# Turning the experts' gated rows through a DRAM scratch and VectorE's 32x32 transposes, with down products two blocks behind

## Chip, cores and metric

One core of one Trainium2 chip runs the kernel, which is written directly for the engines, each with its own instruction list and semaphores. The metric is the device time of one execution in microseconds (us). TensorE (PE) multiplies, VectorE (DVE) and ScalarE (ACT) work element by element, GpSimd (POOL) does small work and software-made transfers, and SyncE (SP) issues transfers.

## Reference, cut to what matters

Two layers follow each other on x (64 batches of 64 tokens, 512 features). The first picks a 64x64 matrix per batch and applies a gated feed-forward net whose weights come from splines. The second adds adapters and a mixture of 8 experts, of which each of the 4096 tokens uses 2:

```python
router_logits = x_flat @ gate_w.T
top_w, sel = jax.lax.top_k(router_logits, TOPK)          # TOPK = 2
top_w = jax.nn.softmax(top_w, axis=-1)
tw = jnp.zeros((n, E)).at[tok_ids, sel].add(top_w)
g = jnp.einsum('nd,efd->enf', x_flat, gate_proj)         # E = 8, F_DIM = 352, D = 512
u = jnp.einsum('nd,efd->enf', x_flat, up_proj)
h = jax.nn.silu(g) * u
eo = jnp.einsum('enf,edf->end', h, down_proj)
out = jnp.einsum('end,ne->nd', eo, tw)
...
x = x + ffn_2(adapters(x))
```

Only the experts' part is touched by the change.

## The kernel before, in words

The first stages (up to about 680 us) compute the first layer, the adapters and the router, and write each token's row, its token number and its two shares to `rows_dram`, sorted by expert. The last stage, `experts`, goes over 71 blocks (`BLOCKS`) of 128 rows. A block has one expert. Its weights sit in one of three `slots`; SP loads the next expert into a slot that is done with.

For block j the work is:

- ACT issues four transfers of the block's rows, `fetch_z(j)` (L1823), four blocks ahead. The rows arrive so that DVE's transpose of 32x32 squares, `turn(j)` (L1881), writes the turned block to a bank.
- The turned block is split into a rounded high part (`high_z`, L1844, ACT) and a low rest (`low_z`, L1885, DVE).
- PE does `gate_up(j)` (L1760): 24 products of 352 columns, in three passes (high by high, high by low, low by high), into the banks GATE and UP.
- ACT takes the silu of GATE (`gate`, L1838), and DVE multiplies it with UP into `hid` (`multiply`, L1894).
- PE turns `hid` by three products with the identity (`transpose_h`, L1773) into the bank HT; ACT and DVE split HT (`high_h` L1834, `low_h` L1889).
- PE does `down(j)` (L1781): 9 products of 512 columns. It comes after `gate_up(j+1)`, so it lags by one block.
- DVE reads the small tile `meta` (L1828 fetches it), computes the block's share (`set_share`, L1900, three tiny operations) and weighs the result (`weigh`, L1911). POOL adds it to `out` by an indirect transfer (`scatter`, L1732), one at a time.

Each engine works in the order of its own `body`. For ACT (L1848) this is `high_h(j-1)`, `high_z(j+1)`, `gate(j)`, `fetch_z(j+4)`, `fetch_meta(j)`. For DVE (L1920) it is `low_h(j-1)`, `turn(j+1)`, `low_z(j+1)`, `multiply(j)`, `set_share(j-1)`, `weigh(j-1)`. For PE (L1802) it is `transpose_h(j-1)`, `gate_up(j)`, `down(j-1)`. A wait in such a list holds back all that stands behind it on that engine; on ACT this covers its transfers too, since the same queue issues them.

Of the kernel before, what the change touches and what calls it, by code (L numbers as in the profile page):

```python
# [16 lines left out]
P = 128  # L17
# [42 lines left out]
FC = 3  # L60
# [182 lines left out]
def build(nc, io):  # L243
    kc = {k: v for k, v in io.items() if k.startswith("c_")}
    dram = lambda n, s, d=F32: nc.dram_tensor(n, s, d, kind="Internal").ap()
    late_dram = [dram(f"late_dram{l}", [P, NT, TILE_W]) for l in range(2)]
    rows_dram = dram("rows_dram", [NE * REGION * P, WIDE])
# [6 lines left out]
    with top:  # L254
# [132 lines left out]
        experts(nc, alloc, sem, psum, ident, small, idle, slots, weights_loaded, load_expert, rows_dram, out,  # L387
# [1270 lines left out]
def experts(nc, alloc, sem, psum, ident, small, idle, slots, weights_loaded, load_expert, rows_dram, out,  # L1658
# [3 lines left out]
    with ExitStack() as scope:  # L1662
        sb = alloc(scope)
        z_quads = [sb(f"z_quads{r}", [P, QUADS, P]) for r in range(AHEAD)]
        meta = [sb(f"meta{b}", [P, META]) for b in range(2)]
# [4 lines left out]
        silu_g, hid = sb("silu_g", [P, FD]), sb("hid", [P, FP])  # L1670
        ht_hi, ht_lo = sb("ht_hi", [P, FC, P], F32R), sb("ht_lo", [P, FC, P], F32R)
# [5 lines left out]
        z_loaded, meta_loaded = [sem(f"ex_z_loaded{r}") for r in range(AHEAD)], [sem(f"ex_meta_loaded{b}") for b in range(2)]  # L1677
        z_turned, zt_high, zt_low, ht_high, hid_set = (sem(n) for n in ("z_turned", "zt_high", "zt_low", "ht_high", "hid_set"))
        part_set, share_set, scatter_set, added = (sem(n) for n in ("part_set", "share_set", "scatter_set", "added"))
# [4 lines left out]
        def quads(zt):  # L1684
            return zt[:, :, :].rearrange("p k (a n) -> p k a n", a=QUADS)
# [8 lines left out]
        with nc.Block() as block:  # L1694
            @block.sync
            def _(sp):
# [8 lines left out]
                for e in range(SLOTS, NE):  # L1705

                    blocks = sp.value_load(ctl[0:1, END_AT + e - SLOTS:END_AT + e - SLOTS + 1], min_val=1, max_val=BLOCKS)
                    sp.wait_ge(filled[HT], blocks + 1)
# [3 lines left out]
                for b in range(2):  # L1712
                    sp.wait_ge(meta_loaded[b], 16 * ((BLOCKS - b + 1) // 2))
# [3 lines left out]
            def _(pool):  # L1717
                nc.gpsimd.memset(hid[:, :], 0.0).then_inc(hid_set, 1)
# [8 lines left out]
                def set_scatter(j, n, b):  # L1727
                    pool.wait_ge(meta_loaded[b], 16 * (n + 1))
                    alone()
                    nc.gpsimd.tensor_copy(scatter_at[b][:, :], meta[b][:, 0:1]).then_inc(scatter_set, 1)  # L1730

                def scatter(j, n, b, first):  # L1732

                    if not first:
                        pool.wait_ge(added, 16 * j)
                        alone()
# [3 lines left out]
                    alone()  # L1740
# [14 lines left out]

            @block.tensor
            def _(pe):
                pe.wait_ge(hid_set, 1)

                def gate_up(j, b, slot):  # L1760

# [226 lines left out]
```

## Time and profile before

| | |
|---|---|
| median of 3 runs | 1149.09 us (1147.99 to 1153.04) |
| the profiled execution, its own time | 1151.42 us |
| its span, first to last instruction | 1149.7 us |
| PE, DVE, ACT, POOL busy | 92%, 60%, 41%, 57% of the span |
| `experts`, first to last `transpose_h` | 691.0 to 1134.5 us |

The page gives busy times for the whole span, a mean over stages with different limits. The change touches the last stage alone, so this stage's own rows are the ones to read: its period for each block, what each engine does in a period, and where it waits. In the rows a `q` behind an engine's name (ACTq) marks instructions that its queue issues; for a transfer the duration is that of the issue, not of the data's way.

### The profile page before, as it was taken

To read this page: it belongs to the slowest core of one execution; us is meant where nothing else is said; L and a number is where in the kernel's file an instruction comes from. 1 tells how busy PE (TensorE), PEld (TensorE's weight loads), DVE (VectorE), ACT (ScalarE), POOL (GpSimd) and SP (SyncE) were. 2 spreads that over 40 slices of the span, in tenths; PEclk is the share of its full clock that TensorE was granted. 3 is DMA by queue.
4 is the path that set the end of the run, shared out by engine and by line. 5 is a ranking of instruction groups with operands and counts; after the bars stand their busy time and mean duration, and the time that the engine had idled before them with its cause. 6 is when DMAs were issued, how large, how long until landed. Compare 5 with 4: busy or idle time off the path is not lost. (4 is left out here: it accounts for less than half of the span.)

```text
span 1149.7 us, 35580 instructions
## 1 busy us (share of the span) xinstructions
PE 1056.2 (92%) x12060; PEld 977.3 (85%) x12061; DVE 692.7 (60%) x1478; ACT 474.0 (41%) x964; POOL 653.4 (57%) x889
## 2 busy tenths in 40 slices
PE   2679999999999999779999929999999999999995
PEld 1679999999999999669999928998999999999994
DVE  8946666677766666447566715555555555555553
ACT  3246767777766776433334212222222222222221
POOL 6568999999999999403646322333333333333333
PEclk9758999999999999869999959999999999999998
DMA  6053554555555455346878567586767676754454
GB/s 260 1 163 123 187 180 163 199 201 176 186 194 180 164 184 167 126 145 196 278 244 266 163 212 190 82 238 122 198 124 196 130 190 136 185 91 78 87 82 65
DMA packets 126611, 188.31 MB, mean 164 GB/s; under 512 B 26040, under 2 KB 89656, under 8 KB 123104
## 3 DMA queue, kind: packets, MB, share of 16 engines
q1 hardware_dynamic: 57408, 130.43, 33.9%
q0 software_dynamic: 16432, 36.78, 16.4%
q10 hardware_dynamic: 52736, 20.64, 7.4%
q8 instruction: 21, 0.34, 0.1%
q14 instruction: 14, 0.11, 0.0%
HBM read 108.37 MB, written 81.83 MB: 165 GB/s over the span
## 5 line engine op out<-in xcount | busy, mean ns | idle before, releaser
L1725 POOL TENSOR_TENSOR idle<-small 128x1 f32<-128x1 f32 x212 | 70.8, 337 | 275.9 <-DMA out<-result,scatter_at 191.5
L1768 PE MATMUL banks<-slots,zt_hi 128*128 x568 | 189.6, 334 | 22.2 <-DVE zt_lo L1887 22.2
L1770 PE MATMUL banks<-slots,zt_lo 128*128 x568 | 184.3, 325 | 0.0
L1769 PE MATMUL banks<-slots,zt_hi 128*128 x568 | 184.3, 325 | 0.0
L962 POOL TENSOR_TENSOR in_lo<-inner,in_hi 128x512 fp32r<-128x512 f32 x128 | 164.5, 1292 | 29.9 <-ACT in_hi L1110 29.6
L1199 DVE TENSOR_TENSOR inner<-silu,banks 128x512 f32<-128x512 f32 x128 | 87.9, 687 | 112.9 <-ACT silu L1105 109.9
L1836 ACT ACTIVATE ht_hi<-banks 128x384 fp32r<-128x384 f32 x71 | 35.0, 493 | 254.9 <-PE banks L1778 247.6
L1741 POOL DMA_INDIRECT out<-result,scatter_at x71 | 111.7, 1573 | 28.1 <-issue 26.4
L1768 PEld LDWEIGHTS banks<-slots,zt_hi 128*128 128x128 f32 x568 | 107.8, 190 | 22.4 <-issue 22.4
L956 POOL TENSOR_TENSOR f_lo<-f_sum,f_hi 128x256 fp32r<-128x256 f32 x128 | 110.9, 887 | 3.8 <-ACT f_hi L1101 3.8
L1105 ACT ACTIVATE silu<-banks 128x512 f32<-128x512 f32 x128 | 76.3, 596 | 76.9 <-PE banks L1031 75.7
L1769 PEld LDWEIGHTS banks<-slots,zt_hi 128*128 128x128 f32 x568 | 107.9, 190 | 0.0
L1770 PEld LDWEIGHTS banks<-slots,zt_lo 128*128 128x128 f32 x568 | 107.8, 190 | 0.0
L1110 ACT ACTIVATE in_hi<-inner 128x512 fp32r<-128x512 f32 x128 | 80.5, 629 | 40.9 <-DVE inner L1199 36.3
L1917 DVE TENSOR_TENSOR result<-banks,share 128x512 f32<-128x512 f32 x71 | 49.1, 691 | 75.9 <-DMA out<-result,scatter_at 51.4
L1031 PE MATMUL banks<-f_hi,gu_hi 64*128 64x256 f32 x512 | 87.4, 336 | 5.9 <-DVE inner L1199 3.0
L1788 PE MATMUL banks<-slots,ht_hi 128*128 x213 | 84.2, 395 | 1.3 <-DVE ht_lo L1891 1.3
L1189 DVE TENSOR_REDUCE f_sum<-banks 128x256 f32<-128x512 f32 x128 | 82.1, 682 | 5.3 <-PE banks L1017 4.9
L1790 PE MATMUL banks<-slots,ht_lo 128*128 x213 | 84.4, 396 | 0.0
L1047 PE MATMUL banks<-in_hi,down_hi 32*128 32x256 f32 x1024 | 83.7, 316 | 0.6 <-POOL in_lo L962 0.6
L1789 PE MATMUL banks<-slots,ht_hi 128*128 x213 | 84.0, 394 | 0.0
L1846 ACT ACTIVATE zt_hi<-banks 128x512 fp32r<-128x512 f32 x72 | 43.1, 599 | 92.2 <-DVE banks L1883 92.1
(255 smaller groups left out, 3148.7 us busy)
## 6 DMA issues: line engine op xcount, KB each, us to landing
late_dram<-split_part SPq DMA_DIRECT2D x32, 816.0 KB, 5.1
slots<-late_dram SPq DMA_DIRECT2D x24, 1088.0 KB, 5.9
z_quads<-rows_dram ACTq DMA_DIRECT2D x286, 64.0 KB, 3.3
raw_part<-in_late_w SPq DMA_DIRECT2D x16, 816.0 KB
x_t<-in_x_t SPq DMA_DIRECT2D x16, 512.0 KB, 3.6
x_both<-in_x_tok SPq DMA_DIRECT2D x16, 512.0 KB, 5.8
x_both<-in_x_res SPq DMA_DIRECT2D x16, 512.0 KB, 3.3
x1t_dram<-x_both SPq DMA_DIRECT2D x16, 512.0 KB, 6.0
```

Of the source, the lines that this page charges most:

```text
L956: nc.gpsimd.tensor_tensor(f_lo[:, g, :], f_sum[g % F_SUMS][:, :], f_hi[:, g, :].bitcast(F32), ALU.subtract).then_inc(f_done, 1)
L962: nc.gpsimd.tensor_tensor(in_lo[:, cs, :], inner[u % 2][:, :, :], in_hi[:, cs, :].bitcast(F32), ALU.subtract).then_inc(in_done, 1)
L1031: ins = nc.tensor.matmul(gu_bank[:, h, m * TILE:(m + 1) * TILE], w[rows, m, cols], f[rows, u, :], start=(i == 0), stop=(i == 2))
L1047: ins = nc.tensor.matmul(out_bank[r][:, cols], w[rows, c, :], x[rows, c, :], start=(c == 0 and i == 0), stop=(c == IC - 1 and i in (2, 4)) ...
L1199: nc.vector.tensor_tensor(inner[u % 2][:, :, :], silu[u % 2][:, :, :], gu_bank[:, :, TILE:2 * TILE], ALU.mult).then_inc(gu_drained, 1)
L1741: nc.gpsimd.indirect_dma_start(out, bass.IndirectOffsetOnAxis(ap=scatter_at[b][:, 0:1], axis=0), result[b][:, :], None, compute_op=ALU.add ...
L1768: nc.tensor.matmul(psum[bank][:, 0:FD], zt_hi[b][:, k, :], w_high, start=(k == 0), stop=False)
L1769: nc.tensor.matmul(psum[bank][:, 0:FD], zt_hi[b][:, k, :], w_low, start=False, stop=False)
L1770: ins = nc.tensor.matmul(psum[bank][:, 0:FD], zt_lo[b][:, k, :], w_high, start=False, stop=(k == DK - 1))
L1788: nc.tensor.matmul(psum[OUT[b]][:, :], ht_hi[:, f, :], w_high, start=(f == 0), stop=False)
L1789: nc.tensor.matmul(psum[OUT[b]][:, :], ht_hi[:, f, :], w_low, start=False, stop=False)
L1790: ins = nc.tensor.matmul(psum[OUT[b]][:, :], ht_lo[:, f, :], w_high, start=False, stop=(f == FC - 1))
```

## The change

`hid` no longer goes through PE. ACT stores it to a scratch in DRAM (`store_h`, 128 x 4 pieces of 96 numbers, 384 bytes each), POOL reads it back in another order (`read_h`, 128 pieces of 1536 bytes), and DVE turns it in 32x32 squares into the bank HT (`turn_h`). Then `high_h` and `low_h` split it as before. The scratch, `hid`, `hid_quads`, `ht_hi` and `ht_lo` have two buffers each, `meta` four. `down` lags `gate_up` by two blocks, `weigh` by three. For the rows to come in the order that this needs, `quads` now writes `zt_hi` and `zt_lo` with "(n a)" where "(a n)" stood: neighbours in a write lie four numbers, 16 bytes, apart. The same holds for `ht_hi` and `ht_lo` (`h_quads`). The down weights' rows are reordered on the host to fit.

```diff
+    hid_dram = dram("hid_dram", [2, QUADS, P, FC * QUAD])
...
         def quads(zt):
-            return zt[:, :, :].rearrange("p k (a n) -> p k a n", a=QUADS)
+            return zt[:, :, :].rearrange("p k (n a) -> p k a n", a=QUADS)
+        def turned_h():
+            return psum[HT][:, 0:FP].rearrange("p (a f n) -> p a f n", a=QUADS, f=FC)
+        def h_quads(ht):
+            return ht[:, :, :].rearrange("p f (n a) -> p a f n", a=QUADS)
...
# GpSimd
+                def read_h(j, n, b, first):
+                    if not first:
+                        pool.wait_ge(h_turned, j - 1)
+                    pool.wait_ge(hid_stored[b], 16 * (n + 1))
                     alone()
+                    nc.gpsimd.dma_start(hid_quads[b][:, :], hid_dram[b].rearrange("q (n a) w -> (q n) (a w)", a=QUADS)).then_inc(hid_loaded[b], 16)
...
# TensorE
-                def transpose_h(j):
-                    pe.wait_ge(drained[UP], j + 2)
-                    pe.wait_ge(drained[HT], j + 1)
-                    for f in range(FC):
-                        ins = nc.tensor.transpose(psum[HT][:, f * P:(f + 1) * P], hid[:, f * P:(f + 1) * P], ident[:, :])
-                    ins.then_inc(filled[HT], 1)
...
                 def body(j, n, b):
-                    last, now = slot_of(j - 1), slot_of(j)
+                    last, now = slot_of(j - 2), slot_of(j)
                     wait_weights(j)
-                    transpose_h(j - 1)
                     gate_up(j, b, now)
-                    down(j - 1, n - 1 + b, 1 - b, last)
+                    down(j - 2, n - 1, b, last)
...
# ScalarE
+                def store_h(j, n, b, first):
+                    act.wait_ge(drained[UP], j + 2)
+                    if not first:
+                        act.wait_ge(hid_loaded[b], 16 * n)
+                    act.dma_start(hid_dram[b].rearrange("q p w -> p q w"), hid[b][:, :, :]).then_inc(hid_stored[b], 16)
...
-                def body(j, b, r):
-                    high_h(j - 1)
+                def body(j, n, b, r, first):
                     act.wait_ge(filled[UP], j)
                     high_z(j + 1, 1 - b)
                     gate(j)
                     fetch_z(j + AHEAD, r)
-                    fetch_meta(j, b)
+                    store_h(j, n, b, first and j < 2)
+                    high_h(j - 1, n - 1 + b, 1 - b, first and j < 3)
+                    next_meta(j, r, first and j < AHEAD)
...
# VectorE
+                def turn_h(j, n, b):
+                    dve.wait_ge(hid_loaded[b], 16 * (n + 1))
+                    nc.vector.transpose(psum[HT][:, 0:FP], hid_quads[b][:, :]).then_inc(h_turned, 1)
...
                 def body(j, n, b, m, r, first):
-                    low_h(j - 1)
-                    turn(j + 1, m, r)
+                    if not first:
+                        finish(j - 3, n - 1 - (1 - b), 1 - b, m - 1 + (r + 1) // AHEAD, (r + 1) % AHEAD, False)
+                    turn(j + 1, m + (r + 1) // AHEAD, (r + 1) % AHEAD)
                     low_z(j + 1, 1 - b)
-                    multiply(j)
-                    set_share(j - 1, n - 1 + b, 1 - b)
-                    weigh(j - 1, n - 1 + b, 1 - b, first)
+                    multiply(j, n, b, False)
+                    turn_h(j - 1, n - 1 + b, 1 - b)
+                    low_h(j - 1, 1 - b)
+                def finish(j, n, b, m, r, first):
+                    set_share(j, m, r)
+                    weigh(j, n, b, first)
```

The order on ScalarE, in the middle of the loop over blocks, before the change. `ISA` rows are register work for an address, TENSOR_LOAD reads a register from a table, `ex_filled3` is the bank HT filled by PE:

```order
L1846 ACTIVATE zt_hi<-banks 128x512 [waits z_turned]
L1842 ACTIVATE silu_g<-banks 128x352 [waits ex_drained2,ex_filled1]
L1689 ISA [waits z_turned]
L1689 TENSOR_LOAD staging
...
L1692 DMA z_quads<-rows_dram 32x4x128
...
L1821 ISA [waits scatter_set,share_set]
L1821 TENSOR_LOAD staging
...
L1832 DMA meta<-rows_dram 128x4
L1836 ACTIVATE ht_hi<-banks 128x384 [waits ex_filled3]
```

The same place of the changed kernel; `ex_drained2` is the product that fills `hid`:

```order
L1870 ACTIVATE zt_hi<-banks 128x4x4x32 [waits z_turned]
L1866 ACTIVATE silu_g<-banks 128x352 [waits ex_drained2,ex_filled1]
L1705 ISA [waits z_turned]
L1705 TENSOR_LOAD staging
...
L1708 DMA z_quads<-rows_dram 32x4x128
...
L1847 DMA hid_dram<-hid 128x4x96 [waits hid_loaded1,ex_drained2]
L1853 ACTIVATE ht_hi<-banks 128x4x96 [waits down_done,h_turned]
L1700 ISA [waits scatter_set,share_set]
```

The store of `hid` has come in between the four fetches and `ht_hi`, and the fetch of `meta` now stands behind `ht_hi`. `ht_hi` waits for DVE's turn in place of PE's.

The order on VectorE at the same place, before the change:

```order
L1891 TENSOR_TENSOR ht_lo<-banks,ht_hi 128x384 [waits ht_high]
L1883 STREAM_TRANSPOSE banks<-z_quads 128x512 [waits ex_z_loaded2]
L1886 REGISTER_ALU
L1887 TENSOR_TENSOR zt_lo<-banks,zt_hi 128x512 [waits zt_high]
L1898 TENSOR_TENSOR hid<-silu_g,banks 128x352 [waits ex_filled2,ex_drained1]
```

and of the changed kernel:

```order
L1919 STREAM_TRANSPOSE banks<-hid_quads 128x384 [waits hid_loaded0]
L1915 TENSOR_TENSOR ht_lo<-banks,ht_hi 128x4x96 [waits ht_high]
L1934 ISA [waits ex_meta_loaded3]
L1934 SCALAR_TENSOR_TENSOR share_parts<-meta,staging 128x1
L1935 SCALAR_TENSOR_TENSOR share_parts<-meta,staging 128x1
L1937 TENSOR_TENSOR share<-share_parts 128x1 [waits part_set]
L1945 REGISTER_ALU [waits down_done,share_set]
L1946 TENSOR_TENSOR result<-banks,share 128x512 [waits added]
L1907 STREAM_TRANSPOSE banks<-z_quads 128x512 [waits ex_z_loaded3]
```

The turn of the next rows (`banks<-z_quads`) stood right behind `ht_lo`; now the three share operations and the weighing stand between the two. The turn of `hid` stands ahead of `ht_lo`.

On GpSimd the read of the scratch is put ahead of each block's index copy and scatter:

```order
L1741 TENSOR_TENSOR idle<-small 128x1 [waits hid_stored1,h_turned]
L1749 DMA hid_quads<-hid_dram 128x384
L1741 TENSOR_TENSOR idle<-small 128x1 [waits ex_meta_loaded3]
L1754 CAST scatter_at<-meta 128x1
L1741 TENSOR_TENSOR idle<-small 128x1 [waits ex_drained5,scatter_set]
L1762 REGISTER_ALU
L1741 TENSOR_TENSOR idle<-small 128x1 [waits added]
L1764 DMA out<-result,scatter_at 4224x512
```

Of these rows the first two are new; the rest was there, with the wait for the last scatter (`added`) ahead of the wait for the result.

## Rows read from the trace of the kernel before

**Rows 1.** The page's busy times, the whole span: busy us (share) x instructions.

```profile
PE 1056.2 (92%) x12060; PEld 977.3 (85%) x12061; DVE 692.7 (60%) x1478; ACT 474.0 (41%) x964; POOL 653.4 (57%) x889
```

**Rows 2.** Busy times by stretch: length, engines' busy (count), PEclk, DMA share, GB/s.

```profile
880.00:940.00 60.00, 60.00 (x345) 55.03 (x344) 33.70 (x79) 13.51 (x28) 21.34 (x49) 1.00 0.70 160
```

**Rows 3.** One line's instructions (`transpose_h`): count, duration ns, first and last start.

```profile
L1778 PE MATMUL banks<-ident,hid x213: 270/272/325, 691.0 to 1134.5; 128*128 128x128 f32 x107
```

**Rows 4.** Timeline of PE at 906 us: start, duration, instruction.

```profile
906.30 0.40 PE L1790 MATMUL banks<-slots,ht_lo 128*128 x1
906.53 0.49 PE L1778 MATMUL banks<-ident,hid 128*128 128x128 f32 x3
906.78 0.41 PE L1768 MATMUL banks<-slots,zt_hi 128*128 x1
```

**Rows 5.** Timeline of ACT over one block; in brackets the idle time ahead.

```profile
1014.66 0.49 ACT L1836 ACTIVATE ht_hi<-banks 128x384 fp32r<-128x384 f32 x1 [3.47 <-PE banks L1778]
1016.41 0.60 ACT L1846 ACTIVATE zt_hi<-banks 128x512 fp32r<-128x512 f32 x1 [1.26 <-DVE banks L1883]
1016.91 0.46 ACT L1842 ACTIVATE silu_g<-banks 128x352 f32<-128x352 f32 x1
1017.42 1.87 ACTq L1692 DMA_DIRECT2D z_quads<-rows_dram  x4
1020.15 0.36 ACTq L1832 DMA_DIRECT2D meta<-rows_dram  x1
1021.11 0.49 ACT L1836 ACTIVATE ht_hi<-banks 128x384 fp32r<-128x384 f32 x1 [3.74 <-PE banks L1778]
```

**Rows 6.** Timeline of DVE and POOL in the same block.

```profile
1014.51 0.69 DVE L1917 TENSOR_TENSOR result<-banks,share 128x512 f32<-128x512 f32 x1 [1.29 <-DMA out<-result,scatter_at]
1015.19 0.56 DVE L1891 TENSOR_TENSOR ht_lo<-banks,ht_hi 128x384 fp32r<-128x384 f32 x1
1015.66 0.72 DVE L1883 STREAM_TRANSPOSE banks<-z_quads 128x512 f32<-128x512 f32 x1
...
1019.01 0.21 DVE L1905 SCALAR_TENSOR_TENSOR share_parts<-meta,staging 128x1 f32<-128x1 f32 x1
...
1019.39 0.16 DVE L1908 TENSOR_TENSOR share<-share_parts 128x1 f32<-128x1 f32 x1
...
1015.97 1.58 POOL L1741 DMA_INDIRECT out<-result,scatter_at  x1 [0.47 <-issue]
```

**Rows 7.** Who waited for whom in `experts`: us in total, times, longest.

```profile
POOL idle L1725 <- DMA meta<-rows_dram: 40.1, 16, 3.9
...
DVE result L1917 <- DVE share L1908: 0.2, 1, 0.2
```

**Rows 8.** The page's transfer issues: count, KB each, median us to landing.

```profile
z_quads<-rows_dram ACTq DMA_DIRECT2D x286, 64.0 KB, 3.3
...
out<-x_tok SPq DMA_DIRECT2D x32, 256.0 KB, 5.7
...
out<-result,scatter_at POOLq DMA_INDIRECT x71, 5.1
...
z_quads<-rows_dram SPq DMA_DIRECT2D x14, 64.0 KB, 2.0
...
cond_w<-in_cond_w,cond_now POOLq DMA_INDIRECT x34, 2.8
```

**Rows 9.** Duration in ns (min/median/max) of issues with 512 and with 128 pieces.

```profile
L1334 SPq DMA_DIRECT2D out<-x_tok x32: 348/828/2765, 508.8 to 637.0; - x32
...
L950 POOL DMA_INDIRECT cond_w<-in_cond_w,cond_now x32: 939/969/1398, 58.8 to 437.7; - x32
```

**Rows 10.** Timeline of the program's end: the last up product, and the last scatter.

```profile
1131.98 0.32 PE L1770 MATMUL banks<-slots,zt_lo 128*128 x1
...
1141.79 1.58 POOL L1741 DMA_INDIRECT out<-result,scatter_at  x1 [0.39 <-issue]
```

More of the change, by code:

```diff
@@ L386, in build @@
         layer.close()
-        experts(nc, alloc, sem, psum, ident, small, idle, slots, weights_loaded, load_expert, rows_dram, out,
+        experts(nc, alloc, sem, psum, ident, small, idle, slots, weights_loaded, load_expert, rows_dram, hid_dram, out,
                 ctl, expert_f, ctl_ready)
@@ L1655, in _, with experts @@
                 nc.vector.tensor_copy(ctl[:, 0:PAD_AT], ctl_f[:, 0:PAD_AT]).then_inc(ctl_ready, 1)
-def experts(nc, alloc, sem, psum, ident, small, idle, slots, weights_loaded, load_expert, rows_dram, out,
+def experts(nc, alloc, sem, psum, ident, small, idle, slots, weights_loaded, load_expert, rows_dram, hid_dram, out,
             ctl, expert_f, ctl_ready):
@@ L1664, in experts @@
         z_quads = [sb(f"z_quads{r}", [P, QUADS, P]) for r in range(AHEAD)]
-        meta = [sb(f"meta{b}", [P, META]) for b in range(2)]
+        meta = [sb(f"meta{r}", [P, META]) for r in range(AHEAD)]
         share_parts, share = sb("share_parts", [P, 2]), sb("share", [P, 1])
@@ L1669, in experts @@
         zt_lo = [sb(f"zt_lo{b}", [P, DK, P], F32R) for b in range(2)]
-        silu_g, hid = sb("silu_g", [P, FD]), sb("hid", [P, FP])
-        ht_hi, ht_lo = sb("ht_hi", [P, FC, P], F32R), sb("ht_lo", [P, FC, P], F32R)
+        silu_g, hid = sb("silu_g", [P, FD]), [sb(f"hid{b}", [P, QUADS, FC * QUAD]) for b in range(2)]
+        hid_quads = [sb(f"hid_quads{b}", [P, FP]) for b in range(2)]
+        ht_hi = [sb(f"ht_hi{b}", [P, FC, P], F32R) for b in range(2)]
+        ht_lo = [sb(f"ht_lo{b}", [P, FC, P], F32R) for b in range(2)]
         result = [sb(f"result{b}", [P, D]) for b in range(2)]
@@ L1717, in _ @@
             def _(pool):
-                nc.gpsimd.memset(hid[:, :], 0.0).then_inc(hid_set, 1)
+                for b in range(2):
+                    nc.gpsimd.memset(hid[b][:, :, :], 0.0).then_inc(hid_set, 1)
                 places = [0]
@@ L1863, in _ @@
                 fetch_z(AHEAD, 0)
[L1864 to L1871 removed]
+                store_h(0, 0, 0, True)
+                body(1, 0, 1, 1, True)
+                body(2, 1, 0, 2, True)
+                body(3, 1, 1, 3, True)
+                for j in range(4, 7):
+                    body(j, j // 2, j % 2, j % AHEAD, False)
+                with act.Fori(1, (BLOCKS - 3) // AHEAD) as k:
                     for i in range(3, 3 + AHEAD):
[L1873 to L1874 removed]
+                        body(AHEAD * k + i, AHEAD // 2 * k + i // 2, i % 2, i % AHEAD, False)
+                high_h(BLOCKS - 1, (BLOCKS - 1) // 2, 0, False)
             @block.vector
```

156 lines of the change are left out of this document (85 added, 71 removed).

## The prediction

> **What bounds the kernel now.** I read first the page's busy times: PE is busy for 92% of the span, no other engine for more than 60% [rows 1]. The change is in the last stage alone, so the second view is the table by stretch: between 880 and 940 us PE is busy for 60.00 of 60.00 us at a granted clock of 1.00, while DVE needs 33.7, ACT 13.5 and POOL 21.3 us [rows 2]. PE is the bound of this stage, and every other engine has spare time as a sum. The length of a block comes from the line of the turns on PE: 213 of them are 71 blocks, the first at 691.0 and the last group at 1134.5 less 0.25, so 443.3 us for 70 periods, 6.33 us each [rows 3].
>
> Sums hide one thing. ACT and DVE wait for each other inside a block, each in the order of its own list, and these hand-overs add up. The timelines of ACT and DVE over one block show this round [rows 5, 6]: `ht_hi` starts at 1014.66, `ht_lo` at 1015.19 (0.53 later), the turn of the next rows at 1015.66 (0.47), `zt_hi` at 1016.41 (0.75), the first fetch is issued at 1017.42 (1.01, silu and the register loads are in it), the four issues take 1.87, to 1019.29, and the issue of `meta` ends at 1020.51 (1.22). The sum is 5.85 us, and the next `ht_hi` starts at 1021.11. The profile shows 3.74 us of idle time ahead of it, but ACT's queue was issuing through most of that; only 0.60 us is spare. The row does not show it, yet this round is second in line behind PE's 6.33.
>
> **What the change removes.** The three turns of a block on PE: they start at 906.53, the next product at 906.78, so 0.25 us a block [rows 4]. PE then needs 6.33 - 0.25 = 6.08 us. The waits of PE between `gate_up` and `down` were already nil, so the greater lag of `down` buys PE nothing more by itself. The fetch of `meta` leaves the round, since it now stands behind `ht_hi`: 1.22 us less, 4.63 left.
>
> **What it adds to the round of ACT and DVE.** The order rows show two things that enter it.
>
> (a) The store of `hid` stands between the fourth fetch and `ht_hi`. No row stores 512 pieces from ACT's queue. The nearest is the store of x_tok from SP's, also 512 pieces: its issue took 0.35 us at least and 0.83 in the median, while many stood in a row [rows 9]; the issue of `meta` took 0.36 [rows 5]. I take 0.5, since only fetches of 128 pieces stand ahead, and 0.1 for the two hand-overs. Bounds 0.35 and 0.83.
>
> (b) The three share operations and the weighing now stand between `ht_lo` and the turn of the next rows, on which `zt_hi` waits. From the first share operation to the last is 0.38 us (1019.01 to 1019.39), that one takes 0.16 [rows 6], the weighing waited 0.2 for it the one time that nothing else was later [rows 7], and from the weighing to the next operation is 0.68 (1014.51 to 1015.19) [rows 6]. Together 1.42 us. Before, they ran while DVE waited for PE or a scatter; that cover is gone, because they now stand behind an operation that ACT releases late.
>
> The round is 4.63 + 0.6 + 1.42 = 6.65 us (6.5 to 7.0 by the bounds of the issue). It is longer than PE's 6.08 and than the 6.33 of before, and it needs no slow transfer to be so. DVE's own sum is no bound: 33.7 us in 60 is 3.5 a block, and a turn of 384 columns adds about 0.6.
>
> **A second round, over two blocks, with the scratch.** The store of block j must have landed and been read back before DVE's turn of it, and that turn stands ahead of `ht_hi(j)` and all that follows, up to the store of block j+2. Its terms:
>
> - the store to landing, 3.3 us, as for the fetches of 64 KB on the same queue (the store has 192 KB, but in as many pieces as the four together); the bounds are 2.0, the fetches that met little else, and 5.7, the stores of x_tok [rows 8];
> - POOL's small operation and the issue's start, about 0.2 + 0.47 [rows 6];
> - the read to landing, 2.8 us, as the gather of `cond_w` from POOL, whose 0.97 us of issue is in it; bounds 2.0 and the 5.1 of the scatter [rows 8, 9];
> - the turn of `hid` to `ht_hi`, 0.6 (0.75 for a turn of 512 columns [rows 5, 6]);
> - from `ht_hi` to the next store: 0.53 + 0.47 + 1.42 + 0.75 + 1.01 + 1.87 + 0.05 = 6.1.
>
> The sum is 13.5 us for two blocks, 6.7 for one (5.7 and 9.1 by the bounds). So both rounds stand at about 6.7, and I take 6.7. The round over two blocks has no slack then, so late transfers show in full. In the stretches in which SP loads an expert, POOL waited 16 times for the 2 KB of `meta`, 40.1 us in all, 2.5 each [rows 7]. If the store came 2.5 late in 16 blocks, half of it would show, 20 us; the fetches' median of 3.3 holds those stretches already, so I take a third, 7 us.
>
> **POOL, queues and weights.** The read stands ahead of the index copy and the scatter. A block's work there is 1.0 for the read, 1.58 for the scatter and some 2 for the rest, 4.6 of 6.7 us, and the wait for the store ends before the weighing is due; no term. SP's load of an expert starts one block later, under two experts' work; no term. The doubled buffers cost nothing in time.
>
> **The end.** Before, the scatter of the last block starts 9.5 us after the last product of `gate_up` is done (1132.30 to 1141.79) [rows 10]. Now nothing covers the way over DRAM: product 0.6, store 0.2 + 3.3, POOL 0.7, read 2.8, turn and split 1.7, share and weighing of the last block but one 1.4 (they stand behind the split), its scatter after 0.7, landing after 5.1 [rows 8], and 0.8 to the last scatter: 17.3. That is 8 us more.
>
> **Sum.** 70 x (6.7 - 6.33) = +26, the loads +7, the end +8: +41 on the 1151.42 us of the profiled execution, 1192. This execution lay 2.3 over the median, so the median should be 1190.
>
> **Weighed against the Trainium skill.** `zt_hi`, `zt_lo`, `ht_hi` and `ht_lo` are now written 16 bytes apart. No row of before has such a write; the nearest, with contiguous ones, are 0.60 for `zt_hi` and 0.56 for `ht_lo` [rows 5, 6], so the cost lies between nothing and as much again. I take nothing, the end that the nearest rows have, and keep the other for the rivals. SBUF — State Buffer, section "Door 1: The DMA port swizzle", says that SBUF has lines of 16 bytes and that at least two accesses must fall in a line for full rate; by it each of these writes would pay. No run here shows it yet; its result is the second rival.
>
> **Rivals.**
>
> - *Faster: neither round binds.* If the store's issue and the hand-overs are hidden in the queue and the round stays under 6.08, PE sets the time: 70 x -0.25 = -17.5, the end +8, 1142 for the execution, 1140 for the median. For it: DVE, ACT and POOL have much spare time as sums. Against it: the round is built from start times, and its parts stand in program order. It decides from a round of 6.2 down, where the gain outweighs the end. Chance 0.12.
> - *Slower still: strided writes at half rate.* In the round `ht_hi` adds 0.5, `ht_lo` 0.55 and `zt_hi` up to 0.6: 8.3 us, 70 x 2.0 = +138, with the end about 1300. At a third of this cost it is 1235. Chance 0.1.
> - *About the same.* A round of 6.2 to 6.3 with a short end: 1143 to 1155. Chance 0.08.
> - *The way over DRAM is long.* With 4.5 for the store and 4.0 for the read the second round is 15.9, 8.0 a block: 70 x 1.6 = +112, with the end 1270. For it: 384-byte pieces into DRAM have no row, and the scatter shares the engines. Chance 0.15.
> - *My forecast,* a block of 6.5 to 7.2. Chance 0.55.
>
> **Range and chances.** What a measurement of this kernel can tell from no change is about 0.5%, 5.7 us. The forecast's own range is 6.5 without the loads' term to 7.2 with it: 70 x 0.17 + 8 = 20 to 70 x 0.87 + 15 = 76, so 1169 to 1225 for the median. To leave out no more than two in ten I reach down to 1157 (hand-overs 0.15 shorter) and up to 1255, half way into the long ones. Faster 0.12, same 0.08, slower 0.80.
>
> **What would show it.** PE should wait at the first product of `gate_up` for `zt_lo`, some 0.6 us a block, where it had no wait. `ht_hi` should start right behind the store's issue; if it waits for the turn of `hid` instead, the second round binds, and DVE should then wait for `hid_quads`. The block should measure 6.7 us, and up to 8 in the loads. `zt_hi` should still take 0.60, or the second rival is true. I am wrong if ACT is idle ahead of `zt_hi` with its turn long done, or if PE stays busy throughout.

## The result, and the profile after

The changed kernel took 1265.95 us in the median of four runs (1260.48 to 1272.74), the kernel before on the same chip 1151.07 us (1147.99 to 1154.06). The ratio is 1.0986, with a 95% interval of 1.0943 to 1.1029: slower by nearly 10%. The forecast was 1190 and the range ended at 1255. The direction held, the size did not.

The experiments below ran on other chips, where the kernel before took 1144 to 1159 us, so they are compared by their ratio to it; the changed kernel was not run again there and keeps its 1.0986. One hundredth of the kernel before is 11.5 us.

The page's busy times of the changed kernel, to be held against [rows 1]:

```profile
PE 1054.1 (84%) x11847; PEld 955.6 (76%) x11848; DVE 772.6 (61%) x1549; ACT 530.0 (42%) x964; POOL 708.3 (56%) x1032
```

PE has the 213 turns less to do, and 8 points less of the span. DVE has gained 80 us and ACT 56 us of busy time. The table by stretch, first for the stretch of [rows 2], then for a late one in which no expert is loaded:

```profile
880.00:940.00 60.00, 47.59 (x244) 41.27 (x244) 33.51 (x67) 15.61 (x21) 22.54 (x53) 0.94 0.77 187
1180.00:1240.00 60.00, 48.81 (x261) 42.90 (x260) 38.21 (x74) 18.70 (x25) 25.47 (x59) 1.00 0.67 129
```

No engine is busy for more than 49 of 60 us. What binds is a chain of hand-overs. In the first stretch the granted clock is 0.94 as well, where before it was 1.00 and PE never paused. In the later one it is 1.00, so the clock is not what makes a quiet block long.

**How long a block takes.** The lines of `gate_up`'s first product and of `ht_hi` give the first and last start of each, before and after (count, duration min/median/max in ns, first and last start):

```profile
L1768 PE MATMUL banks<-slots,zt_hi x568: 318/323/654, 683.3 to 1131.7; 128*128 x190
L1836 ACT ACTIVATE ht_hi<-banks x71: 491/493/494, 691.6 to 1134.8; 128x384 fp32r<-128x384 f32 x71
```

```profile
L1793 PE MATMUL banks<-slots,zt_hi x568: 317/323/654, 681.4 to 1233.4; 128*128 x190
L1853 ACT ACTIVATE ht_hi<-banks x71: 842/852/873, 703.5 to 1243.7; 128x384 fp32r<-128x384 f32 x71
```

From the first to the last product it was 448.4 us and is 552.0: 103.6 more. From the last product to the end of the span it was 18.0 and is 25.3: 7.3 more. The start lies 1.9 earlier, and the sum is the span's +109.0. The distances between two starts of `ht_hi`, worked out from its 71 records, split the 103.6: their median was 6.27 us and is 7.09, 70 x 0.82 = 57 us; what single blocks have above that median, less what others are below it, was 4 us in all and is 44, 40 us (the same count is meant wherever "above the median" stands below); the remaining 7 are the start, where the first `ht_hi` comes 22.1 us after the first product (8.3 before), less what it comes later behind the last product too (7.2).

**A quiet block.** The timelines of ACT and DVE of the changed kernel over one block, with nothing loaded:

```profile
1187.61 0.85 ACT L1853 ACTIVATE ht_hi<-banks 128x384 fp32r<-128x384 f32 x1 [1.98 <-DVE banks L1919]
1191.28 1.08 ACT L1870 ACTIVATE zt_hi<-banks 128x512 fp32r<-128x512 f32 x1 [2.82 <-DVE banks L1907]
1192.12 0.34 ACTq L1708 DMA_DIRECT2D z_quads<-rows_dram  x1
1192.71 1.29 ACTq L1708 DMA_DIRECT2D z_quads<-rows_dram  x3
1194.12 0.39 ACTq L1847 DMA_DIRECT2D hid_dram<-hid  x1
1194.63 0.85 ACT L1853 ACTIVATE ht_hi<-banks 128x384 fp32r<-128x384 f32 x1 [1.98 <-DVE banks L1919]
```

```profile
1188.49 0.86 DVE L1915 TENSOR_TENSOR ht_lo<-banks,ht_hi 128x384 fp32r<-128x384 f32 x1 [1.11 <-ACT ht_hi L1853]
1189.26 0.21 DVE L1934 SCALAR_TENSOR_TENSOR share_parts<-meta,staging 128x1 f32<-128x1 f32 x1
1189.92 0.69 DVE L1946 TENSOR_TENSOR result<-banks,share 128x512 f32<-128x512 f32 x1
1190.53 0.72 DVE L1907 STREAM_TRANSPOSE banks<-z_quads 128x512 f32<-128x512 f32 x1
1192.39 1.09 DVE L1911 TENSOR_TENSOR zt_lo<-banks,zt_hi 128x512 fp32r<-128x512 f32 x1 [1.14 <-ACT zt_hi L1870]
1193.38 0.52 DVE L1927 TENSOR_TENSOR hid<-silu_g,banks 128x352 f32<-128x352 f32 x1
1193.81 0.58 DVE L1919 STREAM_TRANSPOSE banks<-hid_quads 128x384 f32<-128x384 f32 x1
```

From `ht_hi` to `ht_hi` it is 7.02 us: 0.88 to `ht_lo`, 0.77 to the share, 1.27 to the turn, 0.75 to `zt_hi`, 0.84 to the first fetch, 2.00 to the store, 0.51 to the next `ht_hi`. Two things are new. `ht_hi`, `zt_hi`, `ht_lo` and `zt_lo` take 0.85, 1.08, 0.86 and 1.09 us; the contiguous ones took 0.49, 0.60, 0.56 and 0.69. And behind `zt_hi` there are two ways to the next `ht_hi`: ACT's queue is free at 1194.51, with the store issued, and DVE's turn of `hid` ends at 1194.39, behind `zt_lo` and the product. They end 0.12 apart.

**A long block.** The same kernel while SP loads an expert; the load, then POOL, DVE and ACT:

```profile
905.51 20.67 SPq L351 DMA_DIRECT2D slots<-late_dram  x4
```

```profile
906.76 0.41 ACTq L1847 DMA_DIRECT2D hid_dram<-hid  x1
913.95 0.19 POOL L1741 TENSOR_TENSOR idle<-small 128x1 f32<-128x1 f32 x1 [7.25 <-DMA hid_dram<-hid]
914.08 0.59 POOL L1749 DMA_DIRECT2D hid_quads<-hid_dram  x1
919.87 0.59 DVE L1919 STREAM_TRANSPOSE banks<-hid_quads 128x384 f32<-128x384 f32 x1 [6.26 <-DMA hid_quads<-hid_dram]
920.58 0.84 ACT L1853 ACTIVATE ht_hi<-banks 128x384 fp32r<-128x384 f32 x1 [8.22 <-DVE banks L1919]
```

The store takes 7.2 us to land, the read 5.8 from its issue to DVE's turn. DVE stands still for 6.26, and the distance between two `ht_hi` is 13.3. Each of the five loads has one block of 12.6 to 13.6 us and one of 9.3 to 10.4.

The whole of `experts`, who waited for whom (us, times, longest):

```profile
POOL idle L1741 <- DMA hid_dram<-hid: 280.5, 70, 26.2
ACT ht_hi L1853 <- DVE banks L1919: 198.9, 69, 12.5
...
DVE banks L1919 <- DMA hid_quads<-hid_dram: 63.3, 27, 10.1
PE banks L1793 <- DVE zt_lo L1911: 55.4, 57, 1.7
...
PE banks L1804 <- DVE ht_lo L1915: 42.1, 12, 9.0
```

PE waits for `zt_lo` in 57 blocks, 1.0 us each: the quiet round. It waits for `ht_lo` 12 times, 3.5 us each: the loads. POOL's 280.5 us is the largest number but no loss of that size: POOL stands ready early, and a store costs time only where its read then comes late for DVE's turn. PE has no wait for `slots` in the whole of this list, so the longer blocks are not blocks in which the weights were missing.

### The profile page after: what moved, and what is told of

The parts are those of the page before. It is cut to its first block and busy times, and to the rows that moved or that the text cites. A ratio compares the mean times of both kernels' runs of the same rounds, so it can differ in the third digit from the quotient of the medians.

```text
span 1258.7 us, 35627 instructions
## 1 busy us (share of the span) xinstructions
PE 1054.1 (84%) x11847; PEld 955.6 (76%) x11848; DVE 772.6 (61%) x1549; ACT 530.0 (42%) x964; POOL 708.3 (56%) x1032
## 5 line engine op out<-in xcount | busy, mean ns | idle before, releaser
L1741 POOL TENSOR_TENSOR idle<-small 128x1 f32<-128x1 f32 x283 | 55.4, 205 | 329.6 <-DMA hid_dram<-hid 280.5
L1870 ACT ACTIVATE zt_hi<-banks 128x512 fp32r<-128x512 f32 x72 | 78.0, 1083 | 197.6 <-DVE banks L1907 197.6
L1853 ACT ACTIVATE ht_hi<-banks 128x384 fp32r<-128x384 f32 x71 | 60.6, 853 | 205.1 <-DVE banks L1919 203.2
L1764 POOL DMA_INDIRECT out<-result,scatter_at x71 | 116.9, 1647 | 28.8 <-issue 28.5
L1804 PE MATMUL banks<-slots,ht_hi 128*128 x213 | 90.6, 425 | 47.6 <-DVE ht_lo L1915 47.6
L1911 DVE TENSOR_TENSOR zt_lo<-banks,zt_hi 128x512 fp32r<-128x512 f32 x72 | 77.6, 1078 | 81.0 <-ACT zt_hi L1870 71.8
L1915 DVE TENSOR_TENSOR ht_lo<-banks,ht_hi 128x384 fp32r<-128x384 f32 x71 | 60.0, 844 | 74.6 <-ACT ht_hi L1853 74.6
L1806 PE MATMUL banks<-slots,ht_lo 128*128 x213 | 89.0, 418 | 0.0
L1805 PE MATMUL banks<-slots,ht_hi 128*128 x213 | 88.8, 417 | 0.0
L1804 PEld LDWEIGHTS banks<-slots,ht_hi 128*128 128x128 f32 x213 | 43.0, 202 | 59.1 <-issue 52.0
```

The source lines that it names most:

```text
L1764: nc.gpsimd.indirect_dma_start(out, bass.IndirectOffsetOnAxis(ap=scatter_at[b][:, 0:1], axis=0), result[b][:, :], None, compute_op=ALU.add ...
L1804: nc.tensor.matmul(psum[OUT[b]][:, :], ht_hi[b][:, f, :], w_high, start=(f == 0), stop=False)
L1805: nc.tensor.matmul(psum[OUT[b]][:, :], ht_hi[b][:, f, :], w_low, start=False, stop=False)
L1806: ins = nc.tensor.matmul(psum[OUT[b]][:, :], ht_lo[b][:, f, :], w_high, start=False, stop=(f == FC - 1))
L1853: nc.scalar.activation(h_quads(ht_hi[b]), turned_h(), ACT.Copy).then_inc(ht_high, 1)
```

## The experiments

The theory after the result had three parts: strided writes and the early weighing lengthen the round of ACT and DVE; the way over DRAM is a second round close behind it; and the loads make that second round late. The main rival was that the strided writes alone are the loss.

**Strided writes in the kernel before.** `zt_hi` and `zt_lo` only, with the rows of `meta` in the order that goes with them:

```diff
-            return zt[:, :, :].rearrange("p k (a n) -> p k a n", a=QUADS)
+            return zt[:, :, :].rearrange("p k (n a) -> p k a n", a=QUADS)
...
-                    act.dma_start(meta[b][:, :], rows_dram[bass.ds(row_of(j), P), D:D + META]).then_inc(meta_loaded[b], 16)
+                    act.dma_start(meta[b][:, :], rows_dram[bass.ds(row_of(j), P), D:D + META].rearrange("(a n) m -> n a m", a=QUADS)).then_inc(meta_loaded[b], 16)
```

> The kernel before, with only zt_hi and zt_lo written 16 bytes apart (the rows of meta are fetched in the order that this needs). Theory (in-order round of ACT and DVE plus strided writes): the strided writes take 1.08 us each as in the changed kernel, but the round here was 5.85 us against PE's 6.27, and the fetches do not wait for zt_hi to end, so the time stays within 0.5% of before, 1151 to 1157 us. Rival (the strided writes alone cost a block 0.5 us wherever they stand): 70 x 0.5 = +35, 1186 us.

Measured: 1146.78 us, ratio 1.0012 [0.9976, 1.0049]. The page's groups show that the writes did become slow:

```profile
L1887 DVE TENSOR_TENSOR zt_lo<-banks,zt_hi 128x512 fp32r<-128x512 f32 x72 | 77.7, 1079 | 80.5 <-ACT zt_hi L1846 80.5
...
L1846 ACT ACTIVATE zt_hi<-banks 128x512 fp32r<-128x512 f32 x72 | 77.7, 1079 | 89.8 <-DVE banks L1883 89.8
```

Nearly half a microsecond more on each of two engines in every block, and nothing in the time that the interval would show: the round had this much room under PE's 6.27. The price of an operation is only the price of the kernel where its round binds.

**Contiguous writes in the changed kernel.** "(a n)" for "(n a)" in `quads` and `h_quads`. The numbers then stand in another order than the products want, so the output differs; no work is left out.

> The changed kernel with the four split tiles written contiguously again (rows of different tokens are mixed by this, and the output is another). Theory: zt_hi falls to 0.60, ht_hi to 0.49, ht_lo to 0.56 us; of these ht_hi (0.35) and ht_lo (0.30) stand in the round of one block, so a quiet block goes from 7.03 to about 6.4, and the time from 1266 to about 1220. Rival (the two-block way over DRAM binds in quiet blocks too, where each of the two counts once in two blocks): half of it, about 1243.

Measured: 1238.19 us, ratio 1.0822 [1.0772, 1.0872]. It gives back 0.0164, 19 us. The quiet blocks now alternate between 6.3 and 7.0 to 8.4 us, 13.8 for two, and DVE's wait for `hid_quads` grew from 63.3 to this:

```profile
DVE banks L1919 <- DMA hid_quads<-hid_dram: 125.1, 41, 10.9
```

DVE's wait falls in the long block of each pair and is absent in the short one, as a round over two blocks would have it. The rival that the strided writes are the whole loss falls.

**Share and weighing behind the turn.** In the changed kernel, on DVE alone; all is computed:

```diff
+                    turn(j + 1, m + (r + 1) // AHEAD, (r + 1) % AHEAD)
                     if not first:
                         finish(j - 3, n - 1 - (1 - b), 1 - b, m - 1 + (r + 1) // AHEAD, (r + 1) % AHEAD, False)
-                    turn(j + 1, m + (r + 1) // AHEAD, (r + 1) % AHEAD)
```

> The changed kernel with one step moved in the loop on DVE: share and weighing stand behind the turn of the next rows, not ahead of it. Theory: the round of one block loses 1.27 us (7.03 to 5.8), then the two-block way over DRAM binds with about 13.0 / 2 = 6.5 us, so a quiet block takes 6.5 and ht_hi waits for the turn of hid; with the stretches of loads as before, about 1229 us. Rival (strided writes and the store are the whole loss, the order costs nothing since DVE is idle for 40%): no change, 1266.

Measured: 1195.65 us, ratio 1.0461 [1.0419, 1.0503]. It gives back 0.0525, 60 us, more than the 37 that were expected (1229 us). The 1.27 us leave both rounds at once: the median block is 6.10, late in the stage one of 5.7 and one of 6.6 in turn. The expectation had 13.0 us for two blocks; they take 12.3. ACT over two such blocks:

```profile
1110.10 0.85 ACT L1853 ACTIVATE ht_hi<-banks 128x384 fp32r<-128x384 f32 x1 [2.88 <-DVE banks L1919]
1115.80 0.86 ACT L1853 ACTIVATE ht_hi<-banks 128x384 fp32r<-128x384 f32 x1 [1.91 <-DVE banks L1919]
1122.41 0.87 ACT L1853 ACTIVATE ht_hi<-banks 128x384 fp32r<-128x384 f32 x1 [2.84 <-DVE banks L1919]
```

What single blocks have above the median is 46 us, about as before the edit (44). The run with both edits, below, bears on the 0.7 us that two blocks are shorter than expected.

**Short loads.** The changed kernel, with 64 of 2176 columns of each piece loaded for experts 3 to 7 (so most of their weights are left out):

```diff
-                    sp.dma_start(slot[:, at:at + HALF_W // 2], flat[:, (e - EARLY) * HALF_W + h * HALF_W // 2:][:, 0:HALF_W // 2]).then_inc(weights_loaded, 16)
+                    width = 64 if wait else HALF_W // 2
+                    sp.dma_start(slot[:, at:at + width], flat[:, (e - EARLY) * HALF_W + h * HALF_W // 2:][:, 0:width]).then_inc(weights_loaded, 16)
```

> The changed kernel, where the loads of experts 3 to 7 move 64 of 2176 columns each (the other weights are stale and the output is another). Theory: the blocks of 9 to 13 us, two or three for each load, vanish, and every block takes 7.0 to 7.1: 40 us less, 1226. Rival (the long blocks come from the later start of the loads, PE waiting for weights): the same gain, but then a wait of PE for weights must have stood in the changed kernel's trace; and if they come from POOL's own order, no change.

Measured: 1220.01 us, ratio 1.0669 [1.0624, 1.0714]. It gives back 0.0317, 36 us. The median block stays at 7.07, no block is over 8.8, and DVE's wait is down to a third:

```profile
DVE banks L1920 <- DMA hid_quads<-hid_dram: 22.0, 26, 3.6
```

**Short loads in the kernel before.** The same edit.

> The control of e4: the kernel before, where the loads of experts 3 to 7 move 64 of 2176 columns each (stale weights, another output). Theory (the loads hurt only through the way over DRAM): PE binds every block here, so the time stays within 0.5% of before. Rival (the loads slow any version's blocks): about 36 us less, as in e4.

Measured: 1144.87 us, ratio 1.0005 [0.9979, 1.0032]. The loads cost the kernel before nothing that this interval shows (2.4 us at most). They became a cost with the way over DRAM.

**Later weighing and short loads together.**

> e3 and e4 together: share and weighing behind the turn of the next rows, and the short loads (stale weights, another output). Theory (the two effects are separate: an in-order round, and a late way over DRAM): all blocks take 5.7 to 6.5 us in turns, 6.1 in the mean, and the time is that of e3 less 40 us, a ratio to before of about 1.01. Rival (the way over DRAM is long in any block, and e3 only hid it): the long blocks stay, 1.04.

Measured: 1149.07 us, ratio 1.0028 [1.0003, 1.0053]. The median block is 5.99. The page gives the store and the read as

```profile
hid_dram<-hid ACTq DMA_DIRECT2D x71, 192.0 KB, 2.3
hid_quads<-hid_dram POOLq DMA_DIRECT2D x71, 192.0 KB, 3.3
```

The changed kernel's own page has 3.8 for the store. The loads do not make this difference in the median: the later weighing with all its loads has the same 2.3 on its page, and the short loads with the changed order have

```profile
hid_dram<-hid ACTq DMA_DIRECT2D x71, 192.0 KB, 3.6
```

What goes with it is the distance from the scatter's issue on POOL to the store's on ACT. Two blocks of the changed kernel, from the timelines of POOL and ACT; POOL's `idle` operation waits for the landing:

```profile
1178.93 1.65 POOL L1764 DMA_INDIRECT out<-result,scatter_at  x1 [0.44 <-issue]
1179.66 0.40 ACTq L1847 DMA_DIRECT2D hid_dram<-hid  x1
1181.99 0.19 POOL L1741 TENSOR_TENSOR idle<-small 128x1 f32<-128x1 f32 x1 [1.41 <-DMA hid_dram<-hid]
...
1184.74 1.65 POOL L1764 DMA_INDIRECT out<-result,scatter_at  x1 [0.15 <-issue]
1187.09 0.40 ACTq L1847 DMA_DIRECT2D hid_dram<-hid  x1
1190.85 0.18 POOL L1741 TENSOR_TENSOR idle<-small 128x1 f32<-128x1 f32 x1 [4.47 <-DMA hid_dram<-hid]
```

A store 0.73 us behind the scatter's start lands in 2.3 us, one 2.35 us behind it in 3.8. Worked out from the records in the same way, of the changed kernel's blocks away from the loads 21 have a distance of up to 1.1 us, with a median landing of 2.5, and 25 a longer one, with 4.0 (3.6 to 4.5). With the later weighing 38 of 41 have the short distance, and their median is 2.4. So this edit shortened the two-block round by more than its 1.27 us. That the scatter's own data delay the store is the likely reading; no run moved the scatter alone.

The Trainium skill (DMA: Bandwidth & Descriptors, section "Anatomy of one DMA — SWDGE (gpsimd) path") gives a transfer from GpSimd 2.0 us and its bytes at 436 GB/s, an estimate of 2.45 us for these 192 KB. The read, which goes this way, took 3.3, with 0.6 of issue in it; the store, which ACT issues, took 2.3 close behind the scatter. The 7.2 us of the long block is outside that rule.

**No scratch, later weighing.** GpSimd moves `hid` from SBUF to SBUF in four transfers, and ACT stores nothing. Nothing is left out.

```diff
-                    pool.wait_ge(hid_stored[b], 16 * (n + 1))
+                    pool.wait_ge(drained[UP], j + 2)
                     alone()
-                    nc.gpsimd.dma_start(hid_quads[b][:, :], hid_dram[b].rearrange("q (n a) w -> (q n) (a w)", a=QUADS)).then_inc(hid_loaded[b], 16)
+                    for q in range(QUADS):
+                        nc.gpsimd.dma_start(hid_quads[b][q * QUAD:(q + 1) * QUAD, :], hid[b][:, q, :]).then_inc(hid_loaded[b], 16)
...
-                    store_h(j, n, b, first and j < 2)
```

> A version meant to beat both: as e3, and hid goes in four transfers of 32 partitions each from POOL's queue straight to hid_quads, with no store to DRAM and nothing of it in ACT's queue; everything else and the output as in the changed kernel. Theory: one landing in place of two, so neither round binds (one block 5.3, two blocks about 9.6), PE binds with 6.08 us in all blocks, and the long blocks shrink to a few us: 1130 to 1140, a ratio of 0.985 to 0.995. Rival (POOL becomes the bound: 4 issues of 0.6 and their starts, index copy and scatter add up to 5.8 us, and the scatter's own landing of 5.1 stands behind): 6.5 to 7 a block, a ratio of 1.02 to 1.05.

Measured: 1161.88 us, ratio 1.0138 [1.0075, 1.0201]. The gain over the kernel before did not come. The table by stretch shows where it is not lost:

```profile
1060.00:1120.00 60.00, 60.00 (x335) 55.88 (x334) 45.68 (x90) 23.18 (x31) 49.41 (x104) 1.00 0.66 122
```

Quiet blocks are bound by PE again, at 5.88 us (6.27 before), and POOL has 49.4 of 60 us, so the rival of a POOL bound is false there. But the loads still put 36 us into ten blocks, in which DVE waits for `hid_quads`:

```profile
DVE banks L1918 <- DMA hid_quads<-hid: 46.3, 17, 6.5
```

Worked out: 70 x 0.39 = 27 us won by the median; 36.5 less 4.0 lost in the loads, and 8.7 for the first `ht_hi`, at 700.3 where it was 691.6. That is +14, and the spans differ by 14.2 (1163.9 and 1149.7).

**No scratch, the changed kernel's order on DVE.**

> As e7 but with DVE's order of the changed kernel (share and weighing ahead of the turn of the next rows). Theory: the round of one block binds alone, 7.03 less the store's issue and its hand-over of 0.5, so 6.5 us in quiet blocks with almost no long blocks: a ratio of about 1.015. Rival (the way over DRAM was the whole loss): the same as e7.

Measured: 1204.2 us, ratio 1.0518 [1.0472, 1.0564]; I had expected 1.015. The median block is 6.87, though no store is issued and no way over DRAM exists. DVE shows why (ACT's `zt_hi` starts at 1062.58, the next `ht_hi` at 1065.73):

```profile
1063.68 1.09 DVE L1910 TENSOR_TENSOR zt_lo<-banks,zt_hi 128x512 fp32r<-128x512 f32 x1 [1.14 <-ACT zt_hi L1871]
1064.68 0.51 DVE L1926 TENSOR_TENSOR hid<-silu_g,banks 128x352 f32<-128x352 f32 x1
1065.11 0.59 DVE L1918 STREAM_TRANSPOSE banks<-hid_quads 128x384 f32<-128x384 f32 x1
```

The way through `zt_lo`, the product and the turn is 3.15 us from `zt_hi` to `ht_hi`. With the store's issue in ACT's queue it was 3.35. My expectation had only counted ACT's queue. The loads cost this kernel little: its blocks hold 6.5 us above the median, where the direct kernel with the later weighing holds 36 with the same transfers. Its round is 1.0 us longer than PE's need, and late transfers can hide in that: DVE waits 9.3 us for `hid_quads` in all, where it was 46.3. No direct kernel was run with short loads, so for these two the loads' part is read from the traces.

**The same with contiguous writes.** As above, "(a n)" for "(n a)"; the output differs, no work is left out.

> The direct version with VectorE's order of the changed kernel (median round 6.87 us, ratio 1.052), and the splits zt_hi, zt_lo, ht_hi and ht_lo written contiguously, as in the kernel before; the numbers then stand in another order than the products want, so the output differs, and nothing else is left out. Here no way over DRAM stands behind the round of ScalarE and VectorE, so the strided writes must show in full. Theory (in this round ht_hi, ht_lo, zt_hi and zt_lo each pay 0.3 to 0.5 us, 1.1 on ScalarE's route and 1.5 on VectorE's): the round falls under PE's own 5.9 us a block, the median block is 5.9 to 6.0 and the ratio 0.99 to 1.00. Rival (the strided writes cost only what the contiguous scratch version gave back, 0.19 us a block): median 6.7, ratio 1.04.

Measured: 1166.69 us, ratio 1.012 [1.008, 1.016]. The median block is 5.90 and PE is the bound:

```profile
1060.00:1120.00 60.00, 60.00 (x336) 56.00 (x335) 41.12 (x91) 15.17 (x32) 49.43 (x104) 1.00 0.66 124
```

Here the same edit gives back 0.97 us a block, where with the scratch it gave 0.19. The median came out as the theory said. The ratio did not, 1.012 for 0.99 to 1.00, since I had left out the loads, 26 us above the median, and the later first `ht_hi`.

**Paced loads.** Three kernels, each with the loads in eight pieces of 544 KB, one for each block that `down` has finished. All is computed.

```diff
+                    if paced is not None and 4 * l + h:
+                        sp.wait_ge(down_done, paced + (4 * l + h))
+                    sp.dma_start(slot[:, at:at + part], flat[:, (e - EARLY) * HALF_W + h * part:][:, 0:part]).then_inc(weights_loaded, 16)
```

The direct kernel with the later weighing:

> The direct version with the later weighing (no scratch in DRAM, four SBUF to SBUF transfers from GpSimd), and the loads of experts 3 to 7 cut in eight pieces of 544 KB in place of four of 1088 KB, one for each block that down has finished in place of one behind the other. All is computed. Its unpaced form took 1161.9 us, with quiet blocks of 5.88 us and 36.5 us of blocks over the median, all of them in stretches with a load. Theory (a transfer that meets one 1088 KB piece after another comes late past the slack of the round; a smaller piece and a pause between two leave it in time): most of the 36.5 goes, 1130 us, ratio 0.988. Rival (the loads take their bandwidth from the small transfers whenever they run, so that spreading them spreads the loss): 1155 to 1165, ratio 1.01.

Measured: 1164.43 us, ratio 1.0051 [1.0026, 1.0077], against 1.0138 unpaced. The changed kernel:

> The changed kernel with nothing else altered but the loads of experts 3 to 7, cut in eight pieces of 544 KB, one for each block that down has finished. All is computed. Theory (late transfers add to the round over two blocks, which has almost no slack): a piece delays one transfer by less, but there is little slack to take it, so about half of the 36 us that the shortened loads gave back: 1238 us, ratio 1.083. Rival (only the back-to-back load is harmful): 1222, ratio 1.068. Second rival (spread loss): 1257, ratio 1.099.

Measured: 1278.75 us, ratio 1.1023 [1.0955, 1.1091], against 1.0986. With the later weighing over the scratch:

> The version with share and weighing behind the turn of the next rows, still over the scratch in DRAM, with the loads paced in the same way. All is computed. Unpaced it took 1195.7 us, with short loads 1149.1. Theory: its round over two blocks has some 0.9 us of slack a block more than the changed kernel's, so a larger part of the 46 us goes, to 1165 us, ratio 1.018. Rival (only the back-to-back load is harmful): 1152, ratio 1.005. Second rival (spread loss): 1195, ratio 1.045.

Measured: 1208.0 us, ratio 1.0402 [1.032, 1.0484], against 1.0461. The pieces of the first of these loads are now issued over 57.4 us, where the four of the load shown above took 20.7:

```profile
776.13 57.43 SPq L353 DMA_DIRECT2D slots<-late_dram  x8
```

Pacing spreads the late blocks and does not remove them: in the changed kernel 25 blocks are now over 7.5 us where 16 were, and they hold 59 us above the median, not 44. The theory that only pieces back to back do harm falls. Only the direct kernel, whose round has slack, seems to gain; its two intervals just touch (1.0077 and 1.0075).

Side by side, ratio (median block):

| | changed order on DVE | weighing later |
|---|---|---|
| over DRAM, strided | 1.0986 (7.09) | 1.0461 (6.10) |
| over DRAM, contiguous | 1.0822 (6.91) | |
| over DRAM, strided, short loads | 1.0669 (7.07) | 1.0028 (5.99) |
| direct, strided | 1.0518 (6.87) | 1.0138 (5.88) |
| direct, contiguous | 1.0120 (5.90) | |

No version beat the kernel before. A lag of one block more for `turn_h` and `down`, which would give the transfers another 5.9 us, wasn't tried.

## Why the prediction was right, and where it was wrong

**PE no longer the bound: right.** PE waits at the first product for `zt_lo`, 1.0 us in 57 blocks, as the last part of the prediction asked for (0.6 was named). PE's own need without the turns was put at 6.08; the direct kernels measure 5.88 and 5.90 a block at 60.00 of 60.00 us busy. What PE could have won was 0.4 a block, not 0.25. In the kernel before the first product behind the turns held PE for 0.24 us, to the next product's start, and the others 0.16 (medians of the records); the count from the turns' start to the first product leaves this out. The 6.33 that the prediction started from was a mean, with the longer blocks in it; the median was 6.27.

**The round of ACT and DVE, 6.65: right in its mechanism, short by 0.37.** Term by term against the quiet block: the store with its hand-overs was put at 0.6 and is 0.63 (0.12 ahead, 0.39 the issue, 0.12 behind). Share and weighing were 1.42 and are 1.27. `zt_hi` to the first fetch was 1.01 and is 0.84. The failed step is the term of the strided writes, taken at nothing: `ht_hi` adds 0.35 (0.53 to 0.88), `ht_lo` 0.30 (0.47 to 0.77). Sum: 6.65 - 0.15 - 0.17 + 0.65 + 0.04 of rounding and issue = 7.02. It was the step "I take nothing, the end that the nearest rows have". The nearest rows were contiguous and said nothing on a stride.

The second rival had the mechanism and too high a price. It put `ht_hi`, `ht_lo` and `zt_hi` at 1.6 us in the round. Measured, they are 1.7 to 1.8 times as long in ACT (852 and 1083 ns for 493 and 599) and 1.5 to 1.6 times in DVE (844 and 1078 for 557 and 691), and `zt_hi` adds nothing on ACT's own way, since the first fetch is issued 0.84 after its start. The Trainium skill (SBUF — State Buffer, section "Door 1: The DMA port swizzle") asks for at least two accesses in a line of 16 bytes for full rate; the trace agrees that such a pattern costs, with these durations. DVE's two operations also read `zt_hi` and `ht_hi` with this step, so for DVE the runs do not part the write from the read.

**A way that the prediction did not have.** `zt_lo`, the product and the turn of `hid` on DVE lead to the next `ht_hi` as well. This way came out within 0.12 us of ACT's queue, so neither the store's issue nor, with the scratch, the stride can be taken away alone for its full price. The prediction's 0.5 for the store bought only 0.2 when it was removed (7.09 to 6.87).

**The two-block round, 6.7: right that it stands close behind.** The contiguous version shows it: 6.91 in the median and an alternation. That half of the forecast explains why 19 us came back and not 46. The changed kernel shows it as well: from the store at 1187.09 to the one after the next at 1201.00 it is 13.9 us, with 3.8 for the landing, 2.8 from the read's issue to DVE's turn, 0.8 from there to `ht_hi` and 6.4 from `ht_hi` to the store. The prediction's one value of 3.3 for the store stands between the two that were measured, 2.5 and 4.0.

**The loads, +7: wrong, and the dearer of the two failed terms by the edits.** The short loads gave back 36 us where the contiguous writes gave back 19, and the blocks above the median hold 40 more than before. The failed step was to price a load by POOL's wait for 2 KB of `meta`, 2.5 us, and to take a third of its half since the median of 3.3 "holds those stretches already". A median over 286 fetches holds nothing of the few that meet a load. In a load the store took 7.2 us and the read 5.8, 13.0 where 6.8 was reckoned, one after the other and with no slack to take it. The late pair costs 12.6 to 13.6 for one block. The rival of the long DRAM way (4.5 and 4.0 in every block) has the right place; but it holds in the loads alone.

**The end, +8: right.** +7.3 from the last product to the end. The last up product and the last scatter of the changed kernel, from the timelines of PE and POOL:

```profile
1233.68 0.32 PE L1795 MATMUL banks<-slots,zt_lo 128*128 x1
```

```profile
1252.84 1.57 POOL L1764 DMA_INDIRECT out<-result,scatter_at  x1
```

By the prediction's own count it went from 9.5 [rows 10] to 18.8 (1234.00 to 1252.84), where 17.3 was forecast.

**The start: not in the sum.** The way from the first `hid` to the first `ht_hi` is the transfers' in full, and cost 7 us net. The first store alone took 11.3 us to land (688.97 to 700.24), with the four 1088 KB pieces that SP had issued from 682.76 to 684.18 ahead of it.

**The sum by its own terms.** Forecast +26 for the round, +7 loads, +8 end. Measured in the trace +57, +40, +7, and +5 for the start (7 less the 1.9 that `experts` began earlier).

**Shown and argued.** Shown by an edit alone: the strided access (at least 0.97 us a block without the scratch, where PE then binds, 0.19 with it), the early weighing (60 us with the scratch, 44 without), the loads (36 us), the scratch (54 us with the changed order, 37 with the later weighing). Read from the traces only: the start, the end, that the store and the read are each late in a load, and that the store's landing goes with its distance from the scatter. Open: by how much the lower granted clock in the long blocks adds to them, 0.94 in the stretch from 880 to 940 against 1.00, and which of the shared resources delays a transfer there.

## What to carry to other kernels

Ahead of a change that puts operations of two engines in each other's way, add up every way round the cycle, not only the one with the longest queue, and give each a price from a row of the same access pattern; where there is no such row, take half of the bound rather than nothing. A transfer that is waited for inside a cycle must be priced by its landing while the large loads run, since a median over a whole stage hides these, and slack of less than that turns each load into a stall. Work that nobody waits for soon (here the weighing) belongs behind the operation that another engine waits for: moving the turn ahead of it gave back 60 of 115 us, a part of it, as the traces read, since the store then stood closer behind the scatter and landed sooner.

## What the runs showed of the hardware

- A write with a step of 16 bytes between neighbours of 4 bytes, on DVE with one input read in the same step: ACT 128x512 from 599 to 1083 ns, 128x384 from 493 to 852; DVE 128x512 from 691 to 1078, 128x384 from 557 to 844. The turn of 128x512 keeps its 0.72 us.
- A store of 512 pieces of 384 bytes from ACT's queue takes 0.40 us to issue in the median, where `meta`'s 128 took 0.36 in [rows 5]. It lands in 2.5 us when it is issued up to 1.1 us behind the start of the scatter, in 4.0 when it is issued later, and in 7.2 to 8.5 in the long block of a load of 1088 KB pieces. GpSimd's four SBUF to SBUF transfers take 2.8 us to issue together.
- Halving the pieces of a load and pausing between them did not lessen what it costs the small transfers, 1.1023 for 1.0986, though the pieces of a load were issued over 57.4 us in place of 20.7.
